# Cross-attention stage of a decoder kernel: the top-32 cut as one two-slope ScalarE pass, with new orders on TensorE and ScalarE

## What is computed

```python
Q = (x_text @ Wq).reshape(Bb, Tt, H, DH)                  # H = 4 heads of 32
K = (x_vision @ Wk).reshape(Bb, Gg, H, DH)
scores = jnp.einsum('bthd,bghd->bhtg', Q, K) / np.sqrt(DH)
topv, topi = jax.lax.top_k(scores, K_TOP)                 # K_TOP = 32
probs = jax.nn.softmax(topv, axis=-1)
attn = jnp.zeros_like(scores).at[bi, hi, ti, topi].set(probs)
attn_mean = attn.mean(axis=1)
c_t = jnp.einsum('btg,bgd->btd', attn_mean, x_vision @ Wv)
# then: FiLM-in, convolution of the modulated x over 1024 positions, FiLM-out
```

## Time and profile before

| | |
|---|---|
| median of 3 runs | 4655.69 us (4653.27 to 4660.83) |
| profiled execution | 4659.99 us |
| its span | 4658.0 us, mean granted clock 0.926 |
| DVE busy, whole span | 3700.9 us (79%) |
| PE busy, whole span | 4039.2 us (87%) |
| ACT, POOL busy, whole span | 2070.8 us (44%), 2351.6 us (50%) |
| DVE busy, 984 to 2995 us | 1988.75 of 2011.00 us |
| PE busy, 984 to 2995 us | 1841.31 of 2011.00 us, clock 0.94 |

### The profile page before, as it was taken

The page is one execution under the profiler, slowest core; times in us unless marked ns, Lnnn a source line. Parts: engine busy times, 40 slices in busy tenths (PEclk is TensorE's granted clock), DMA queues, the critical chain, the costliest instruction groups (busy, mean ns, idle before and its releaser), DMA issues. The chain is left out here.

```text
span 4658.0 us, 72037 instructions
## 1 busy us (share of the span) xinstructions
PE 4039.2 (87%) x28037; PEld 2944.3 (63%) x28066; DVE 3700.9 (79%) x4865; ACT 2070.8 (44%) x3816; POOL 2351.6 (50%) x2260
## 2 busy tenths in 40 slices
PE   8999995669999999999999999885788998999984
PEld 6777772336666676666766676674566666666652
DVE  5666666869999999999999999772577767766767
ACT  3334332125555555555554555412254454544543
POOL 1111113725666589998889988802333332333320
PEclk9999997769999999999999999897899999999997
DMA  2111114230111111121111111225411111112101
GB/s 84 53 49 46 53 44 166 75 117 28 37 37 51 45 39 42 46 64 30 42 51 63 38 30 39 89 73 181 139 48 52 49 50 53 51 47 61 46 23 38
DMA packets 216421, 276.08 MB, mean 59 GB/s; under 512 B 96899, under 2 KB 144707, under 8 KB 212560
## 3 DMA queue, kind: packets, MB, share of 16 engines
q1 hardware_dynamic: 198674, 216.92, 15.5%
q0 software_dynamic: 17408, 54.56, 3.2%
HBM read 186.44 MB, written 84.98 MB: 58 GB/s over the span
## 5 line engine op out<-in xcount | busy, mean ns | idle before, releaser
L1626 POOL TENSOR_TENSOR c_s<-c_s,c_z 128x2048 f32<-128x2048 f32 x128 | 581.4, 4542 | 358.3 <-ACT c_z L1382 352.0
L1956 PE MATMUL f_p_g<-f_hT,f_w 128*128 128x128 f32 x4096 | 537.6, 295 | 70.4 <-ACT f_gT L2056 55.9
L1192 PE MATMUL c_p_a<-c_diag,c_s 128*128 128x128 f32 x4096 | 526.0, 291 | 75.6 <-ACT c_diag L1396 67.0
L1192 PEld LDWEIGHTS c_p_a<-c_diag,c_s 128*128 128x128 f32 x4096 | 514.3, 207 | 111.7 <-ACT c_diag L1396 82.7
L1956 PEld LDWEIGHTS f_p_g<-f_hT,f_w 128*128 128x128 f32 x4096 | 526.1, 210 | 90.9 <-ACT f_gT L2056 58.8
L1964 PE MATMUL f_p_o<-f_w,f_gT 128*128 128x512 f32 x1024 | 481.8, 592 | 0.0
L1538 DVE TENSOR_TENSOR c_z<-c_s 128x1024 f32<-128x1024 f32 x256 | 456.6, 1783 | 3.7 <-ACT c_s L1371 3.7
L1263 PE MATMUL c_p_m<-c_wf,c_uT 128*128 128x512 f32 x768 | 383.4, 638 | 67.7 <-issue 63.3
L1371 ACT ACTIVATE c_s<-c_p_s 128x512 f32<-128x512 f32 x512 | 282.1, 590 | 293.7 <-PE c_p_s L1183 234.3
L1244 PEld LDWEIGHTS c_p_m<-c_aT,c_vals 128*128 128x128 f32 x3072 | 355.8, 194 | 62.5 <-issue 41.3
L1390 ACT ACTIVATE c_s<-c_s,c_nb 128x2048 f32<-128x2048 f32 x128 | 256.4, 2003 | 286.0 <-POOL c_s L1626 286.0
(11 more groups left out here) (378 smaller groups left out, 8900.9 us busy)
## 6 DMA issues: line engine op xcount, KB each, us to landing
mod_out<-c_fo POOLq DMA_DIRECT2D x32, 512.0 KB, 3.2
f_mr<-mod_out SPq DMA_DIRECT2D x32, 512.0 KB, 4.6
p_ct<-in_ctxT SPq DMA_DIRECT2D x16, 768.0 KB, 4.9
c_vals<-in_ctx SPq DMA_DIRECT2D x4, 3072.0 KB, 12.4
c_kb<-kspec SPq DMA_DIRECT2D x22, 512.0 KB, 5.0
a_xt<-in_xT SPq DMA_DIRECT2D x32, 256.0 KB, 3.2
a_xr<-in_x SPq DMA_DIRECT2D x32, 256.0 KB, 2.6
x<-a_out POOLq DMA_DIRECT2D x32, 256.0 KB, 2.5
```

The lines of the kernel that those rows point to most:

```text
L1192: last = mm(p_a[:, n, :], s[:, j % RING, n * P:(n + 1) * P], diag[:, j % 2, :], start=(h == 0 and n % 4 == 0), stop=(h == NH2 - 1 and n % ...
L1626: pool.tensor_tensor(row, row, low, ALU.subtract).then_inc(cut_ready, 1)
L1956: last = mm(p_g[:, f % 8, :], w1[:, k, f * P:(f + 1) * P], hT[:, k * P:(k + 1) * P], start=(k == 0 and f % 4 == 0), stop=(k == KD - 1 and ...
```

## The change

1. `cut` on GpSimd and the ramp on ScalarE go. `below(j)` rewrites the row in place with a two-slope function (Prelu): the score less the 32nd largest where that isn't negative, and 2^80 times that difference where it is. `weigh(j)` takes the exponential with another bias, `eb`, which a one-column ScalarE operation at the end of `below` makes.
2. VectorE gets `floor(j)`: a one-column operation with two SBUF inputs that keeps the 32nd largest from lying over 1024 under the largest. `z_done` is now reported by `floor`, which stands behind the MAX8 of L1566 and right before the next fold.
3. TensorE's order: `slot(t)` and then `attn(4t)` now stand ahead of `context(t-1, 0)`.
4. ScalarE's order: most steps between the rows' work are moved, as shown.

```diff
-                if t:
-                    context(t - 1, 0)
-                attn(j)
                 if slot_job(t) is not None:
                     slot(t)
+                attn(j)
+                if t:
+                    context(t - 1, 0)
...
-                a(tb[:, par:par + 1], top[:, par, 31:32], ACT.Copy, scale=STEEP).then_inc(tb_ready, 1)
                 at_least(act, w_ready, j - 1)
+                a(tb[:, par:par + 1], top[:, par, 31:32], ACT.Copy, scale=-1.0).then_inc(tb_ready, 1)
                 a(nb[:, par:par + 1], top[:, par, 0:1], ACT.Copy, scale=-SCALE).then_inc(nb_ready, 1)
                 act.wait_ge(tb_ready, j + 1)
-                at_least(act, cut_ready, j)
-                a(low, s[:, j % RING, :], ACT.Relu, bias=tb[:, par:par + 1], scale=-STEEP).then_inc(low_ready, 1)
+                row = s[:, j % RING, :]
+                a(row, row, ACT.Prelu, bias=tb[:, par:par + 1], alpha=STEEP).then_inc(cut_ready, 1)
...
+                a(eb[:, par:par + 1], top[:, par, 31:32], ACT.Identity, bias=nb[:, par:par + 1], scale=SCALE).then_inc(eb_ready, 1)
 
             def weigh(j):
                 act.wait_ge(cut_ready, j + 1)
+                act.wait_ge(eb_ready, j + 1)
                 row = s[:, j % RING, :]
-                a(row, row, ACT.Exp, bias=nb[:, j % 2:j % 2 + 1], scale=SCALE).then_inc(w_ready, 1)
+                a(row, row, ACT.Exp, bias=eb[:, j % 2:j % 2 + 1], scale=SCALE).then_inc(w_ready, 1)
...
+            def floor(j):
+                first, last = top[:, j % 2, 0:1], top[:, j % 2, 31:32]
+                v.scalar_tensor_tensor(last, first, -FAR, last, ALU.add, ALU.max).then_inc(z_done, 1)
...
-                at_least(dve, z_done, j)
                 st.link(fold(j, upper, ALU.max))
                 at_least(dve, sum_done, j - 1)
+                at_least(dve, eb_ready, j - 1)
...
-                    v.max(best[3], row).then_inc(z_done, 1)
-                    st.wait()
-                    st.mark(v.max(nxt[1], lower))
+                    st.behind(v.max(best[3], row))
+                    st.behind(v.max(nxt[1], lower))
+                    floor(j)
...
-            def cut(j):
-                pool.wait_ge(low_ready, j + 1)
-                row = s[:, j % RING, :]
-                pool.tensor_tensor(row, row, low, ALU.subtract).then_inc(cut_ready, 1)
```

More of the change, by code:

```diff
@@ L902, in cross @@
         RING = NH2 + 1
+        FAR = 1024.0
         TILES, LAST = TOK // P, TOK // P * NH2 - 1
@@ L923, in cross @@
         tb = m.sb("tb", [P, 2])
+        eb = m.sb("eb", [P, 2])
         den = m.sb("den", [P, 2])
@@ L971, in cross @@
         p_m = m.ps("p_m", [P, 2, 512])
-        (core_in, film_in, consts, values_in, s_done, s_copied, z_done, nb_ready, tb_ready, low_ready, cut_ready,
+        (core_in, film_in, consts, values_in, s_done, s_copied, z_done, nb_ready, tb_ready, eb_ready, cut_ready,
          sum_done, rd_ready, w_ready, im_ready, diag_ready, attn_done, aT_copied, uT_done, uT_copied,
@@ L979, in cross @@
             m.sem(n) for n in (
-                "core_in film_in consts values_in s_done s_copied z_done nb_ready tb_ready low_ready cut_ready "
+                "core_in film_in consts values_in s_done s_copied z_done nb_ready tb_ready eb_ready cut_ready "
                 "sum_done rd_ready w_ready im_ready diag_ready attn_done aT_copied uT_done uT_copied "
@@ L1293, in _ @@
                     scores(t + 1, 0, 0)
+                if slot_job(t) is not None:
+                    slot(t)
+                attn(j)
                 if t:
                     context(t - 1, 0)
-                attn(j)
-                if slot_job(t) is not None:
-                    slot(t)
                 if more:
@@ L1445, in _ @@
                 more = t + 1 < TILES
-                if t:
-                    below(j - 1)
                 if t > 1:
@@ L1451, in _ @@
                 if t:
+                    below(j - 1)
+                copy_s(t, 1, 1)
+                if t:
                     weigh(j - 1)
                     diagonal(j - 1)
-                copy_s(t, 1, 1)
                 if t > 1:
@@ L1457, in _ @@
                 copy_s(t, 1, 2)
-                below(j)
                 if more:
                     copy_x(t + 1)
-                if t:
-                    copy_a(t - 1)
+                below(j)
                 if more:
@@ L1466, in _ @@
                 copy_s(t, 1, 3)
-                weigh(j)
-                diagonal(j)
+                if t:
+                    copy_a(t - 1)
                 if forward_job(t) is not None:
                     copy_f(t)
+                diagonal(j)
+                weigh(j)
+                if slot_job(t) is not None:
+                    copy_slot(t)
                 below(j + 1)
@@ L1475, in _ @@
                     copy_s(t + 1, 0, 1)
-                if slot_job(t) is not None:
-                    copy_slot(t)
-                diagonal(j + 1)
+                weigh(j + 1)
                 if more:
                     copy_s(t + 1, 0, 2)
-                below(j + 2)
                 if t:
@@ L1486, in _ @@
                     copy_s(t + 1, 0, 3)
-                weigh(j + 1)
-                if not more:
-                    copy_fi(TILES - 2)
+                below(j + 2)
+                diagonal(j + 1)
                 weigh(j + 2)
                 diagonal(j + 2)
+            copy_fi(TILES - 2)
             copy_fo(TILES - 2)
@@ L1570, in _ @@
                     st.link(v.match_replace(row, best[2], row, NEG))
-                    v.max(best[3], row).then_inc(z_done, 1)
+                    st.link(v.max(best[3], row))
+                    floor(j)
             invert(LAST)
@@ L1696, in _ @@
                 j = t * NH2
-                if t:
-                    cut(j - 1)
                 if t > 1:
@@ L1701, in _ @@
                 masked_identity(t)
-                cut(j)
                 if begun and not of_kernel(begun):
@@ L1706, in _ @@
                     transform(t)
-                cut(j + 1)
                 if inverse:
@@ L1711, in _ @@
                     store_mod(t - 2)
-                cut(j + 2)
                 if inverse:
@@ L1717, in _ @@
             modulate(TILES - 2)
-            cut(LAST)
             store_mod(TILES - 2)
```

## The result

The changed kernel takes 4626.49 us (median of 4 runs, 4623.32 to 4627.62) against 4658.26 before in the same series: ratio 0.9931, interval 0.9914 to 0.9949. It is 32 us faster, 0.7%. I had forecast 69 us. The sign held and the time lies in the range, but less than half of the forecast gain came: VectorE got 80 us of waits that I had put at nothing.

The account below looks back on a forecast made before the run. VectorE's search for the 32 largest was taken as the bound. Late tiles -62, early tiles +3, together -59, and the tail -10 made -69: 4655.69 to 4587 us, range 4545 to 4642.

Parts of the forecast that it names:

- What bounds the kernel: All 32 tiles: VectorE's search for the 32 largest sets the pace, busy 64.45 of 65 us in a late tile.
- Cut gone, -69, the other stalls unchanged: VectorE's folds: 3.27 us saved in each of 21 late tiles, 69 us; stalls with the convolution stay at 3.79 per tile.
- Rival (b): VectorE's folds and floors: GpSimd's other work slides to the cuts' places, stalls stay 7.06 us a tile; 4656 us, chance 0.07.
- Floor, 0.07 us each and no stall of its own: New VectorE operation before a fold: 0.07 us each, 0.3 per tile, taking over that fold's stall and adding none.
- rival (c): VectorE's floors: each waits 1.27 us for GpSimd while the fold behind still stalls; +38, 4693 us, chance 0.08.
- z_done later, ScalarE reordered: 1.9 us of cover: ScalarE's copy_s(t,1,3) behind below(4t): ready 4.5 us into the step, fold at 6.5 us, so 1.9 us of cover left.
- TensorE: "I book nothing": TensorE before spectra: stands some 4 us per tile waiting for copy_q; no cost entered in the sum.
- my 57 + 4 = 61: TensorE in a tile: matmuls of about 57 us plus 4 us waiting make 61, just under the late tile's 62.1.
- Rival (a): TensorE sets the pace: 59.4 us busy plus 4.2 waiting make a late tile of 63.6; 4641 us, chance 0.12.
- The tail, -10: End of the stage: attn(127) comes 10.5 us after VectorE's end instead of 20.5, so -10; bounds -4.5 and -12.
- The sum: Whole kernel: -59 for the tiles and -10 for the tail make -69, from 4655.69 to 4587 us.
- The range: Whole kernel: 4545 to 4642 us, the lower end from stalls down to 1.5 a tile; rivals (b) and (c) left out.

Follow-up runs that it names:

- e7: The kernel before the change, with GpSimd's cut made one column wide and all waits and orders kept: 4532.78 us, ratio 0.973.
- e9: e3 without floor, z_done reported by the last round's MAX8 and the bound on the 32nd largest left out: 4541.18 us, ratio 0.975.
- e8: e3 with floor as an operation with one SBUF input and the second value as its per-partition scalar: 4564.89 us, ratio 0.9801.
- e3: The changed kernel with one ScalarE step moved, copy_q(t+1) ahead of below(4t): 4551.37 us, ratio 0.9768.
- e6: The changed kernel, order untouched, with nine extra matmuls (results overwritten) on TensorE before spectra's wait for copy_q: 4540.87 us, ratio 0.9756.
- e1: The changed kernel's operations (two-slope pass, floor, no cut) with TensorE's and ScalarE's orders of before the change: 4582.77 us, ratio 0.9837.

## Why the prediction fell short, step by step

- *What bounds the kernel*: right. Every experiment's time follows VectorE's folds, floors and waits.
- *Cut gone, -69, the other stalls unchanged*: the direction right, the size wrong. e7 measured 120 us of folds. I carried over unchanged the 3.79 us that folds lost to the convolution's operations; with cut gone that went too. That GpSimd's sequence then runs earlier and meets the folds elsewhere is my reading, which no run fixed by itself. In the changed kernel folds and floors exceed their quiet length by 3.5 us in one late tile and 0.3 in the next, 1.9 on the mean and below my lower bound of 2.9. Rival (b), in which the stall only moves, is out.
- *Floor, 0.07 us each and no stall of its own*: right in size, with some luck. 9 us forecast, 10 measured (e9) as a sum of terms that partly cancel, and the stall mostly shared with the fold (e8, e9). Floor did pay at GpSimd's door, with 11 floors over 1 us and the longest 1.455, as the Trainium skill's lock rule (SBUF — State Buffer, "SBUF: two separate sides") says; rival (c) failed because the fold behind it then paid nothing.
- *z_done later, ScalarE reordered: 1.9 us of cover*. Right for the copy that I looked at: no fold waited for c_s. But the list of who waits for below was not complete. The reciprocal of the row stands 6.4 us into VectorE's step and waits for the same below. With below 5 to 9 us late, it is the first to stall.
- *TensorE: "I book nothing"*. This is the step that failed. I had the 4 us gap before spectra and the row that shows a slowed group, 5.47 us for 3.74, yet my 57 + 4 = 61 holds the gap and nothing for the lower clock behind it. Here that clock lasted through spectra, scores, slot and part of attn, cost nearly 9 us, and reached VectorE over copy_slot. Worth 80 us in waits, where I had none; e3 and e6 each take it away. I had also compared TensorE's sum with the length of a tile, which can't show a wait inside it. Rival (a) named TensorE as the bound, and its 4641 lies nearer to the result than my 4587; its late tile of 63.6 us is close to the 64.0 that tiles 12 to 29 take on the mean. But that is in part chance: it had a gap in every tile and no lower clock behind it; what happened is a slow tile, which leaves TensorE late enough that the next has no gap, and so by turns.
- *The tail, -10*: right, -11.
- *The sum*: -126 + 29 + 80 in the search, which is 16 as measured, 11 in the tail and 2 at the start (the first fold at 982.51 against 984.38) make 29; the last 3 us of the 32 lie in the stages behind. Folds and floors gave -97 where I had -59, and hid nearly half of the 80. With the old orders (e1) the operations gave 75, close to the 69 forecast, but as the difference of two errors: folds and floors better by some 50 us, waits for the copy of 39.
- *The range*: its lower end holds a slip. From 4566, stalls of 1.5 instead of 2.9 in 21 tiles are 29 us, so 4537 and not 4545.

That slow tiles alternate because a late TensorE has no gap is read from the timeline alone: from tile 12 to 30 the gap is 3.33 or 3.34 us in every second tile but one (there 1.70, behind an attn already slowed to 4.99 us), and 0 to 0.15 in the others. No run fixed it by itself. Why e6 scattered by 41 us between its runs is open.

## What to carry to other kernels

When one engine is the bound, a reordering of the others is worth only what it hides, but it can cost: list every instruction of the bounding engine that waits for the moved work, down to one-column ones, and count the cover of each. Look for gaps of a few microseconds that a reordering opens on TensorE in front of a long run of matmuls, and price the whole run behind them at the lower clock, not the gap. And don't carry port stalls over to a changed kernel: remove the operation in an experiment and read the folds.

## What the runs showed of the hardware that I had not expected

- Behind 3.33 us idle the granted clock was 0.50 (1.2 GHz) for spectra, scores and slot, 16.3 us from 2487.14 to 2503.40 in which TensorE was busy throughout; spectra and slot took 1.9 times as long, and attn after them was still slowed in part. The clock had fallen within the gap, at 2485.43, and rose at 2505.91, 20.48 us later; each of the ten slow tiles from 12 to 30 has a stretch of this length. The tile's mean granted clock was 0.84.
- 261 useless matmuls made the kernel 86 us faster (e6). The clock of the search was 0.97 instead of 0.91, which took away 79 us of waits in the run traced; 20 us more came from folds and floors that met GpSimd less.
- A one-column VectorE operation with two SBUF inputs took 0.146 us in the median and up to 1.455 us when it met GpSimd's operations; with one SBUF input and a per-partition scalar all 128 took 0.187 to 0.214 us.
- Cutting a GpSimd operation down to one column (e7), which had cost the folds 69 us, gave them 120.
